# GpSimd's list of work reordered: batch 1's scatters without pace, half of batch 2's scatters ahead of the weight parts and a gate step

## What is computed

```python
def _L0_attn_ref(x, w_lhs, w_rhs):
    lhs = x * w_lhs
    rhs = x * w_rhs
    scores = jnp.einsum('nsd,ntd->nst', lhs, rhs)
    attn = jax.nn.softmax(scores, axis=2)
    return jnp.einsum('nst,ntd->nsd', attn, x)

def _L0_ffn_ref(x, router_w, w_fc, b_fc, w_proj, b_proj):
    ...
    logits = xf @ router_w.T
    probs = jax.nn.softmax(logits, axis=-1)
    topk_probs, topk_idx = jax.lax.top_k(probs, TOP_K)
    topk_probs = topk_probs / jnp.sum(topk_probs, axis=-1, keepdims=True)
    combine = jnp.zeros((N, E), dtype=x.dtype).at[jnp.arange(N)[:, None], topk_idx].add(topk_probs)
    h = gelu_new(jnp.einsum('nc,ech->neh', xf, w_fc) + b_fc)
    out = jnp.einsum('neh,ehc->nec', h, w_proj) + b_proj
    y = jnp.einsum('nec,ne->nc', out, combine)
    return y.reshape(B, T, C)

x = x + _L0_attn_ref(_layernorm(x, axis=-1), L0_attn_w_lhs, L0_attn_w_rhs)
x = x + _L0_ffn_ref(_layernorm(x, axis=-1), L0_ffn_router_w, L0_ffn_w_fc, L0_ffn_b_fc, L0_ffn_w_proj, L0_ffn_b_proj)
```

## Time and profile before

| | us |
|---|---|
| median of 3 runs | 371.75 |
| lowest and highest | 371.2, 372.22 |
| the profiled execution, its whole time | 370.49 |
| its span, first to last instruction | 368.7 |
| granted TensorE clock over the span, as a share of full speed | 0.92 |
| busy: PE, DVE, ACT, POOL | 293.3, 222.1, 194.5, 185.7 |

### The profile page before, as it was taken

The page is one execution under the profiler, slowest core; times in us unless marked ns, Lnnn a source line. Parts: engine busy times, 40 slices in busy tenths (PEclk is TensorE's granted clock), DMA queues, the critical chain, the costliest instruction groups (busy, mean ns, idle before and its releaser), DMA issues.

```text
span 368.7 us, 7888 instructions
## 1 busy us (share of the span) xinstructions
PE 293.3 (80%) x2206; PEld 256.7 (70%) x2207; DVE 222.1 (60%) x890; ACT 194.5 (53%) x392; POOL 185.7 (50%) x247
## 2 busy tenths in 40 slices
PE   8989988999769994999699272999999999995000
PEld 3669985889558883788588161999999999995000
DVE  3759788888837887778667022665544544453055
ACT  4445557862635614746588022677776777772000
POOL 7011034543865137488786675456555655566300
PEclk9999999999998999999989776799999999999555
DMA  7920000030010001014213321023322222111198
GB/s 218 431 95 1 2 1 0 3 117 16 22 51 29 4 16 45 29 32 118 75 38 90 81 75 59 30 74 110 89 81 75 80 80 72 45 37 50 48 338 325
DMA packets 16948, 29.37 MB, mean 80 GB/s; under 512 B 3760, under 2 KB 12848, under 8 KB 16656
## 3 DMA queue, kind: packets, MB, share of 16 engines
q1 hardware_dynamic: 12080, 18.40, 15.5%
q0 software_dynamic: 4832, 10.53, 8.6%
HBM read 16.30 MB, written 12.62 MB: 78 GB/s over the span
## 4 chain that ended last, share of the span: by engine, by line
PE 60%; DVE 15%; issue 11%; DMA 4%; POOL 4%; ACT 3%; another core or an unknown queue 2%; SPq 1%; POOLq 0%; ACTq 0%; DVEq 0%
PE av_ps L1295 18%; PE av_ps L1094 12%; DVE neg_piece L1402 6%; PE sc_ps L1276 5%; PE sc_ps L1274 5%; PE sc_ps L1275 5%; DMA raw_proj<-results 3%; PE bank L1262 3%; POOL results L867 2%; PE bank L1079 1%; PE sc_ps L1083 1%; PE bank L1083 1%; PE bank L1070 1%; DVE stats L1445 1%
## 5 line engine op out<-in xcount | busy, mean ns | idle before, releaser
L867 POOL DMA_INDIRECT results<-prob,result_row x78 | 75.2, 964 | 57.1 <-PE sc_ps L1276 35.3
L1295 PE MATMUL av_ps<-raw_proj,raw_fc 128*128 x624 | 80.9, 284 | 10.1 <-issue 10.1
L768 POOL DMA_INDIRECT slots<-stage,slot x64 | 63.1, 987 | 45.7 <-DVE stage L1562 21.9
L1295 PEld LDWEIGHTS av_ps<-raw_proj,raw_fc 128*128 128x128 f32 x624 | 76.8, 200 | 10.6 <-issue 9.9
L1011 ACT ACTIVATE raw_fc<-sc_ps,bfc,scale_down 128x256 f32<-128x256 f32 x156 | 75.3, 570 | 2.3 <-PE sc_ps L1276 2.3
L1094 PE MATMUL av_ps<-h_all,prob 128*128 128x137 f32 x512 | 73.2, 287 | 0.0
L1094 PEld LDWEIGHTS av_ps<-h_all,prob 128*128 128x128 f32 x512 | 67.3, 192 | 3.6 <-DVE res L1430 1.1
L1731 DVE TENSOR_TENSOR h_all<-av_ps,bpr 128x256 f32<-128x256 f32 x39 | 16.6, 425 | 75.3 <-PE sc_ps L1276 43.6
L1003 ACT ACTIVATE h_all<-bank 128x512 f16<-128x512 f16 x39 | 23.2, 597 | 60.1 <-PE sc_ps L1276 32.6
L1274 PE MATMUL sc_ps<-h_all,wfc_hi 128*128 128x256 f16 x156 | 43.7, 280 | 2.7 <-issue 1.8
L1275 PE MATMUL sc_ps<-h_all,wfc_hi 128*128 128x256 f16 x156 | 43.7, 280 | 1.1 <-issue 1.1
(11 more groups left out here) (177 smaller groups left out, 516.7 us busy)
## 6 DMA issues: line engine op xcount, KB each, us to landing
slots_in<-slots SPq DMA_DIRECT2D x39, 132.0 KB
raw_fc<-in_w_fc_dram SPq DMA_DIRECT2D x1, 2048.0 KB, 11.2
raw_proj<-in_w_proj_dram SPq DMA_DIRECT2D x1, 2048.0 KB, 15.4
raw_fc<-results SPq DMA_DIRECT2D x2, 1024.0 KB, 7.1
raw_proj<-results SPq DMA_DIRECT2D x2, 1024.0 KB, 11.7
out_dram<-res SPq DMA_DIRECT2D x4, 512.0 KB, 5.0
res<-in_x_dram SPq DMA_DIRECT2D x3, 512.0 KB, 5.6
results<-prob,result_row POOLq DMA_INDIRECT x78
```

Source lines behind the costliest of these rows:

```text
L768: pool.indirect_dma_start(out=slots[:, :], out_offset=bass.IndirectOffsetOnAxis(ap=slot[:, n, k:k + 1], axis=0), in_=stage[:, b % 2, t, :] ...
L867: pool.indirect_dma_start(out=results[:, :], out_offset=bass.IndirectOffsetOnAxis(ap=result_row[a][:, h:h + 1], axis=0), in_=gated[a][h], ...
L1295: mm = pe.matmul(o, hid[:, a % NH, c, s], wpr[:, e, c, :], start=(c == 0 and h == 0), stop=(c == HC - 1), skip_group_check=True)
```

## The change

Three pieces of POOL's list are moved; no instruction is added or removed on any engine, and the waits taken away are the paces of eleven scatters.

1. In the stretch of batch 3, the scatters 5 to 15 of batch 1 lose their paces. Scatters 5 to 11 stand ahead of `gate_powers` of round 2 and 12 to 15 behind it. Scatters 12 to 15 stood behind `scale_ln2(5)`.
2. The first half of batch 2's scatters (0 to 7) moves up: two ahead of `scale_ln2(5)`, six behind it. They stood behind the three `low_part`, and batch 2's scatters 8 to 15 are now what stands between `scale_ln2(6)`, `scale_ln2(7)` and `gate_powers` of round 4.
3. `gate_powers` of round 3 stood ahead of the three `low_part` and now stands behind them, and so behind the six scatters too.

```diff
--- before.py
+++ after.py
@@ -813,9 +813,14 @@
                     dispatch_max(b - 2)
                     dispatch_next(b - 2, 0)
                 if b == B - 1:
-                    dispatch_max(b - 2)
+
+                    for i in range(len(PACE_OWN), SCATTERS - 4):
+                        dispatch(b - 2, i)
                     gate_powers(ROUNDS_BY[b - 1] - 2)
-                    dispatch_next(b - 2, 0)
+                    for i in range(SCATTERS - 4, SCATTERS):
+                        dispatch(b - 2, i)
+                    for i in range(2):
+                        dispatch(b - 1, i)
                 if b >= 1:
                     scale_ln2(2 * b - 1)
                 if b == 1:
@@ -824,13 +829,15 @@
                     clear_empty()
                     for half in range(2):
                         store_empty(half)
-                if b >= 2:
+                if b == 2:
                     dispatch_next(b - 2, 1)
-                if b >= 1:
-                    gate_powers(ROUNDS_BY[b - 1] - 1)
                 if b == B - 1:
+                    for i in range(2, SCATTERS // 2):
+                        dispatch(b - 1, i)
                     for i in range(EMPTY_PIECES, PIECES):
                         low_part(i)
+                if b >= 1:
+                    gate_powers(ROUNDS_BY[b - 1] - 1)
                 if b >= 1 and b + 1 < B:
                     dispatch_own(b - 1, 0)
                 if b == 0:
@@ -844,16 +851,16 @@
                 if b >= 1 and b + 1 < B:
                     dispatch_own(b - 1, 1)
 
-            for i in range(5):
+            for i in range(8, 10):
                 dispatch(B - 2, i)
             scale_ln2(2 * B - 2)
-            for i in range(5, 11):
+            for i in range(10, 12):
                 dispatch(B - 2, i)
             scale_ln2(2 * B - 1)
-            for i in range(11, 15):
+            for i in range(12, 14):
                 dispatch(B - 2, i)
             gate_powers(len(ROUNDS) - 1)
-            for i in range(15, SCATTERS):
+            for i in range(14, SCATTERS):
                 dispatch(B - 2, i)
```

More of the change, by code:

```diff
@@ L826, in _ @@
                         store_empty(half)
-                if b >= 2:
+                if b == 2:
                     dispatch_next(b - 2, 1)
+                if b == B - 1:
+                    for i in range(2, SCATTERS // 2):
+                        dispatch(b - 1, i)
+                    for i in range(EMPTY_PIECES, PIECES):
+                        low_part(i)
                 if b >= 1:
                     gate_powers(ROUNDS_BY[b - 1] - 1)
-                if b == B - 1:
-                    for i in range(EMPTY_PIECES, PIECES):
-                        low_part(i)
                 if b >= 1 and b + 1 < B:
```

## The result

The changed kernel takes 377.62 us (median of four runs, 374.89 to 378.63), the kernel before beside it 371.48 (370.97 to 372.22): a ratio of 1.0146, 95% interval 1.0095 to 1.0197, so slower by about 1.5%. The forecast was 374.5, the range 369.5 to 381. The profiled execution took 374.89 us with a span of 373.1, against 370.49 and 368.7 before: 4.4 us more. It was the quickest of its four runs.

The account below looks back on a forecast made before the run. The prediction took PE's work to set the time, with PE's signals late during POOL's unbroken scatters. Its terms +6.2 + 1.0 - 4.5 gave +2.7 us on 371.75, so 374.5 us, range 369.5 to 381.

Parts of the forecast that it names:

- What bounds the kernel: PE's work sets the time; its signals arrive late when POOL has scattered without a pause for some 7 us.
- Term A: Batch 3's stretch of attention: without paces fourteen scatters run together and make signals late, +6.2 us (bounds 0 and 9.7).
- first rival: No lag in attention: paces cost nothing, the late round 3 gate 3.4, the expert stage gains 4.5; 370.6 us, chance 0.20.
- Term B: End of attention: round 3's gate behind scatters and low parts makes DVE, then PE wait, +1.0 us (3.4 without lag).
- Term C: Expert stage: half of batch 2's scatters gone, so ACT's 3.32 us wait and 1.15 of PE's `down` go, -4.5 us.
- The sum: Whole kernel: +6.2 + 1.0 - 4.5 = +2.7 us, a forecast of 374.5 us, given chance 0.48.
- long-lag rival: In attention the lag lasts to the end of the scatter run, costing 9.7 us: +6.2 in all, 378.0 us, chance 0.20.

Follow-up runs that it names:

- before_b: The kernel before, unchanged, run again on a chip with late signals: 370.16 us, ratio 1.0003.
- e1_b: The kernel before with only the paces in batch 3's stretch removed, on a chip with late signals: 378.26 us, ratio 1.0223.
- f2_spread_both: The kernel before with batch 0's scatters spread over batch 2's exponentials and batch 3's sixteen over steps 6 to 12, quiet chip: 352.94 us, ratio 1.0388.
- e3_b: The kernel before with batch 0's eleven scatters spread over batch 2's exponentials, on a chip with late signals: 365.65 us, ratio 0.9895.
- after_b: The changed kernel, unchanged, run again on a chip with late signals: 377.97 us, ratio 1.021.
- f3_six_behind: The changed kernel with batch 2's scatters 3 to 8 behind the low parts and the gate of round 3, quiet chip: 336.88 us, ratio 0.9914.
- e3_spread_batch0: The kernel before with batch 0's eleven scatters each behind its own exponential of batch 2, quiet chip: 339.73 us, ratio 0.9999.
- e2_gate_first: The changed kernel with the gate of round 3 moved ahead of the three low parts, quiet chip: 341.17 us, ratio 1.0029.

## Why the prediction was right, and where it was not

**What bounds the kernel** held: the time went where PE's signals are late, and the pauses of the earlier trace rows changed by 0.2 us in all. That these pauses and the lag of the earlier trace rows are one thing was assumed. In attention PE had done its work and the others started 4 us later. In the long pauses PE's own timeline, here of the kernel before, has single matmuls 1.4 us apart that wait for nothing the profile shows:

```profile
205.37 0.27 PE L1295 MATMUL av_ps<-raw_proj,raw_fc 128*128 x1 [1.19 <-issue]
206.81 0.27 PE L1295 MATMUL av_ps<-raw_proj,raw_fc 128*128 x1 [1.17 <-issue]
208.22 0.27 PE L1262 MATMUL bank<-ident,slots_in 128*128 128x128 f16 x1 [1.15 <-issue]
```

So PE itself may get on late there, and not only its signals. (In the second of the two stretches ACT and DVE work 2.4 us each, where the prediction has them do nothing.) No run separates the two, nor says by what way POOL's scatters reach PE.

**Term A** was +6.2, and 6.7 were measured by the turns, then 7.8 and 7.5 on the chip of before_b. e1_b shows that it alone makes the loss. Its size is in part luck, because the comparison of batch 2 with batch 3 left out TensorE's clock. "The same work" between two turns holds for the number of matmuls (101 and 102), not for their time: the paced turns of batch 3 are 17.4 us apart on either kind of chip (18.3 in f2_spread_both) and the undisturbed ones of batch 2 15.6, since PE has stood still for 3.8 us ahead of batch 3's first turn and the clock is down behind that stop (0.54 from 146.3 to 149.5 in the kernel before; over the whole stretch in e3_b 0.90 against 1.00, busy 16.80 us against 15.31). That made ten scatters look like 4.4 us where e3_b measures 5.6. The other error is the scaling by number: fourteen were to cost 14/10 of ten, and between them the traces have 5.6 to 7.3 us for ten and 6.7 to 7.8 for fourteen, so nearly no growth. The two lean against each other. That signals come late behind POOL's scatters was right on this kind of chip, and nothing on the other: the rule "no lag" of the first rival describes the quiet chips to 0.1 us in B, though not its sum of -1.1, which counted C in full.

**Term B** was +1.0, the value 0. The two waits of POOL and DVE worked out as told (the gate made at 175.98, told 177.6), but DVE came later than told. A second lag that the prediction did not have, `neg_rows` at 172.85, pushed it from 175.0 to 176.2, and the gate was in time by 0.2 us. On the quiet chip, where DVE is early, B is 3.48 against 3.4 worked out.

**Term C** was -4.5. The wait of 3.32 us went as told, and the credit was not whole: against the kernel before, the expert start gained 2.9 us in the first pair of traces and 2.6 in the second (38.43 us from table load to pause end against 41.06); only against e1_b, which has no paces either, was it 4.6. (The 1.15 us of C that were put down to PE's `down` "after its pause" are the clock again: 0.62 in that stretch, 1.00 in the one it was compared with.) The step that failed is the one that let the six scatters of batch 2 run at 164 to 171.6 for nothing but their time on POOL. They are a run of their own, and with them the last signals of attention are late (3.90 and 4.26 us of ACT's time, 2.6 of the end of attention by after_b against e1_b, which also differ in the place of the gate). The lag was moved more than it was removed.

**The sum** fits better than its terms. For attention A and B were 7.2, and 7.4 was measured, 6.7 of it in the turns and the rest in the second lag; for the expert start -4.5 stood against -2.9. The profiled executions differ by 4.4 us (forecast 2.7), the medians by 6.1 and, on the chip of before_b, by 7.8 (377.97 against 370.16; 6.8 against the 371.15 of all its runs). So the forecast of 374.5 was 3.1 us low: about half of it is the missing part of C (1.6), the other that the medians lie further apart than the two profiled executions (6.1 - 4.4 = 1.7). The long-lag rival, 378.0, named the time more closely than the forecast, but by an A of 9.7, which no trace shows.

**What I could not have known from one trace** is that A, and C as it was reckoned, belong to one kind of chip. The same edit is 1.5 to 2% slower on one and 0.5% on the other.

## What to carry to other kernels

A pace (a wait that has no data behind it) in a list of indirect DMAs can be worth its place: where the trace shows "remote" waits behind a run of them, break the run up with waits on the consumer's progress. Before a group of scatters is moved, ask of the new place what the run does to signals there, what stands behind it in the queue (here a gate), and which load waits for its last one. A stop of PE costs more than its length where the clock falls behind it: here 4.1 us of standing still brought 2.6 us of slower matmuls, so compare stretches by busy time and granted clock and not by length alone. And measure on more than one chip: the spread of batch 0 gains 1% (0.3 to 1.9) where signals are late and nothing elsewhere, and the order of f3_six_behind gains 0.9% on a quiet chip and is unmeasured on the other kind.

## What the runs showed of the hardware

- The same kernel takes 371 us on some chips and 340 on others. On the first kind ACT and DVE have remote waits of up to 6 us during runs of POOL's indirect scatters in attention, and of up to 11 us in the expert stage; on the second no remote wait shows. Why the chips differ no run here tells.
- The Trainium skill (SBUF — State Buffer, Who interferes with whom) says that DMA never contends with a compute engine. On the quiet chips spacing the scatters otherwise changes nothing (e3_spread_batch0, 0.9999), which agrees; on the chip of before_b it takes 5.6 us out of batch 2 with the same transfers (e3_b). That is no proof against a rule about memory ports, but the rule may not be read as if the place of scatters were free.
- Behind a stop of PE of 4.23 us the granted clock is 0.50, its level of 1.2 GHz, for at least 4.75 us, and a matmul with 512 columns takes 0.63 us instead of 0.40.
- A DVE `tensor_scalar` of 128x4 lasted 3.36 us instead of 0.17 under POOL's `tensor_tensor`, and a cast 1.75 us under POOL's fills. To issue a small result of POOL sooner brought nothing in e2_gate_first, where POOL's next operation held DVE.
